# A transformer block on one core: the router's weights made stationary, and matmuls whose result nobody reads put around a stage change

## The chip, the cores and the metric

The kernel runs on one core of one Trainium2 chip. The metric is the device time of one execution in microseconds (us). Three runs of the kernel before took 631.16, 630.52 and 634.32 us, a median of 631.16 us. The program is one launch; nothing of the computation is done on the host beyond laying out the inputs.

## What is computed

One block on x of shape (2048, 256), all in 32-bit floats:

```python
h = layernorm(x) * (1 + ca) + sa
x = x + ga * attention(h)          # 16 heads of 16, windows of 64 queries on 128 keys
h = layernorm(x) * (1 + cb) + sb
x = x + gb * ffn(h)

# router of ffn, for every token:
g = h @ rg_w.T; u = h @ ru_w.T                 # 16 experts, 256 -> 16 each
scores = abs(u * silu(g)); probs = softmax(scores)
idx = top_k(probs + extra_bias, 4); w = 1 + probs[idx] * extra_scale
# y = sum over the 4 experts of w_e * (silu(h @ wg.T) * (h @ wu.T)) @ wd.T, plus one shared expert
```

The masked softmax of a window runs over the 128 keys of the window's own and the preceding 64 positions. All matrices of the experts are 176 wide, the shared one 352.

## The kernel before, in words

**Three stages**, each a block of its own with an instruction stream for each engine; a block begins when every engine has finished the one before.

1. `project_qkv`: normalises x, transposes it on TensorE, and multiplies by the query, key and value weights in eight groups of 256 tokens. Queries and keys go to DRAM (`q_scr`, `k_scr`) and come back in another layout. TensorE's loop is `for_groups`; at its end it has nothing more to do, while SyncE still waits for the last stores and loads (`qk_st`, `qk0_ld`).
2. `attention_and_routing`: 16 tiles of 128 queries (n = 0 to 15). A program written out by hand sets the order on every engine; there is no planner. For a tile, four times (q = 0 to 3, four heads each), TensorE makes scores with queries as columns (`SB`), VectorE takes the row maxima from them (L908), TensorE transposes the maxima (L1178, tile `Y`), ScalarE copies them (`max_out`, L741), SyncE writes them by a DMA into a row of `MM`, and then TensorE makes the transposed scores (`TB`, L1160 and L1162), ScalarE takes the exponential (`exps`, L781), and TensorE multiplies by the values (`weigh`, L1172, tile `O`). The scores of the next tile are made among these. After that a tile's output is normalised, transposed (`transpose_o`, L1183), split in a high and a low part (`o_hi`, `o_lo`) and projected (`project_out`, by the helper at L109), into the same bank `Y` that takes the transposed maxima.
   Each pair of tiles is routed two pairs later: in an odd tile its normalised rows are transposed (L1196, bank `X`), in the next even tile they are split (`h2_hi`, `h2_lo`), `router` multiplies them by the router's weights, ScalarE takes an exponential (`router_exp`, L764), VectorE goes on (`route_scores`), and in the odd tile after it VectorE chooses the experts and TensorE counts ranks (`ranks`, L1210 and L1211). GpSimd sends the rows to `xs_scr` by indirect DMAs (L144). Even tiles with a router are n = 4, 6, ..., 14, six of them; the last two pairs are routed behind the loop.
3. `experts_and_output`: 96 steps of 128 rows on the experts, then 16 tiles of the shared expert.

**What sets the order around the change.** On ScalarE an even tile is: `h2_hi`, `exps(0)`, `exps(1)`, `o_hi`, `router_exp` part 0, `spread(n + 2)` (L775, it lays out queries for a later tile; only where n is at most 13), `exps(2)`, `max_out(n + 1)`, `spread`, `exps(3)`, `router_exp` part 1. On TensorE it is: scores, `router`, `transpose_o`, `weigh(0)`, `scores_t(2)`, `transpose_max(n + 1)`, `weigh(1)`, `project_out`, `scores_t(3)`, `weigh(2)`, `weigh(3)`, scores. Both engines work strictly in this order. `project_out` waits for `max_out(n + 1)`, since both use the bank `Y`:

```python
            weigh(n, 1)
            if runs(n, 1):
                if more:
                    eng.wait_ge(mt_cp, n + 2)
                project_out(m)
```

The products in high and low parts are made by `three` (L109): high by high, low by high, high by low. The router's twelve matmuls have the tokens as the stationary operand (128 columns of weights loaded for each) and 32 columns of router weights moving.

Of the kernel before, what the change touches and what calls it, by code (L numbers as in the profile page):

```python
# [12 lines left out]
P = 128  # L13
# [25 lines left out]
W_GU, W_DN = KD * 2 * FI, 2 * D  # L39
TB_PAD, TB_COL = 2, 20  # L40
L1_OPS, L2_OPS = 16, 16
R_OPS, P_OPS, RP_OPS = 20, 4, 9
W_EXP = W_GU + W_DN
HW = D + 2 * NE
# [522 lines left out]
        for_groups(eng, group)  # L567


def attention_and_routing(nc, A, T, ctx, own):  # L570


# [3 lines left out]
    def sb(name, shape, dt=F32):  # L576
        return ctx.enter_context(nc.sbuf_tensor(name, shape, dt))
# [7 lines left out]
    def sems(name, n):  # L585
        return [sem(f"{name}{i}") for i in range(n)]

    ident, iota_e, mod, VW, QC, K2, MM = [T[x] for x in ("ident", "iota_e", "mod", "VW", "QC", "K2", "MM")]
    mask_key, mask_qry, tri, r_hl, esc, wo_hl = [T[x] for x in ("mask_key", "mask_qry", "tri", "r_hl", "esc", "wo_hl")]
    half = T["half"]  # L590


    Q2 = [sb(f"Q2_{i}", [VALID + 1, HEADS, 2, CH], F32R) for i in range(4)]
# [13 lines left out]
    xn2 = sb("xn2", [P, 2, D])  # L607
    h2t = sb("h2t", [P, 2, D])
    h2T = sb("h2T", [P, 2, 2, KD, P], F32R)
    rt = sb("rt", [P, 10, 2, NE])  # L610
    rw = sb("rw", [P, 2, 2, NE])
    r_sm = sb("r_sm", [P, 3, 2])
# [29 lines left out]
    ln2_dve, ln2_act, ln2_mod, h2_ready = [sem(x) for x in ("ln2_dve", "ln2_act", "ln2_mod", "h2_ready")]  # L642
    th2_mm, h2T_hi, h2T_lo = sem("th2_mm"), sem("h2T_hi"), sem("h2T_lo")
    x1_st, h2_st = sems("x1_st", 4), sems("h2_st", 2)
    r_mm, r_act, r_dve, r_pool, rank_mm, p_dve = [sem(x) for x in ("r_mm", "r_act", "r_dve", "r_pool", "rank_mm", "p_dve")]
    cnt_mm, cnt_cp, tb, col_mm, step_tab = [sem(x) for x in ("cnt_mm", "cnt_cp", "tb", "col_mm", "step_tab")]
    block = ctx.enter_context(nc.Block())
# [88 lines left out]
    def _(eng):  # L736
# [18 lines left out]
        def h2_hi(p):  # L755
            eng.wait_ge(th2_mm, p + 1)
            eng.activation(h2T[:, 0], X[:, :].rearrange("p (a k x) -> p a k x", a=2, k=KD), ACT.Copy).then_inc(h2T_hi, 1)

        def router_exp(g, part):

            if part == 0:
                eng.wait_ge(r_mm, g + 1)
                v = X[:, 0:4 * NE].rearrange("p (a u x) -> p a u x", a=2, u=2)
                eng.activation(rt[:, 0, :, :], v[:, :, 0, :], ACT.Exp, scale=-1.0).then_inc(r_act, 1)  # L764
            else:
                eng.wait_ge(r_dve, R_OPS * g + 7)
                eng.activation(rt[:, 6, :, :], rt[:, 5, :, :], ACT.Exp).then_inc(r_act, 1)
# [20 lines left out]
        def tile(n, t, e, i):  # L788
            even = t % 2 == 0
            ahead = runs(n, 0, TILES - 3)  # L790
            if even and runs(n, 4):
                h2_hi(e - 2)
            exps(n, 0)
            if ahead and not even:
                spread(n + 2, (t + 2) % 4, 0, e + 1)
            exps(n, 1)
            if runs(n, 1):
                o_hi(n - 1)
            if even and runs(n, 4):
                router_exp(e - 2, 0)  # L800
            if ahead and even:
                spread(n + 2, (t + 2) % 4, 0, e + 1)
            if not even and runs(n, 3):
                normalise_x1(e - 1, (t // 2 + 1) % 2)
            exps(n, 2)
            if runs(n, 0, TILES - 2):
                max_out(n + 1, e + t % 2, (t + 1) % 2)
            if ahead:
                spread(n + 2, (t + 2) % 4, 1, e + 1)
            exps(n, 3)  # L810
            if even and runs(n, 4):
                router_exp(e - 2, 1)

        each_tile(tile)
        h2_hi(PAIRS - 2)
        o_hi(LAST)
        router_exp(PAIRS - 2, 0)
        router_exp(PAIRS - 2, 1)

# [2 lines left out]
        load_raw(eng, A, T, FIRST + 4, NE - 1, T["w_rest"])  # L822
        normalise_x1(PAIRS - 1, 1)
        h2_hi(PAIRS - 1)
        router_exp(PAIRS - 1, 0)
        router_exp(PAIRS - 1, 1)

# [71 lines left out]
    def _(eng):  # L899
# [66 lines left out]
        def route_scores(g):  # L966

            c = Chain(eng, r_dve, R_OPS * g)
            v = X[:, 0:4 * NE].rearrange("p (a u x) -> p a u x", a=2, u=2)

            eng.wait_ge(r_act, 2 * g + 1)
            c.mark(eng.tensor_scalar(rt[:, 1, :, :], rt[:, 0, :, :], 1.0, None, ALU.add)).wait()
            c.mark(eng.reciprocal(rt[:, 2, :, :], rt[:, 1, :, :])).wait()
            c.mark(eng.tensor_tensor(rt[:, 3, :, :], v[:, :, 0, :], rt[:, 2, :, :], ALU.mult)).wait()
            c.mark(eng.tensor_tensor(rt[:, 4, :, :], v[:, :, 1, :], rt[:, 3, :, :], ALU.mult)).wait()
            c.mark(eng.scalar_tensor_tensor(out=rt[:, 9, :, :], in0=rt[:, 4, :, :], scalar=-1.0, in1=rt[:, 4, :, :],
                                            op0=ALU.mult, op1=ALU.max)).wait()
            c.mark(eng.tensor_reduce(r_sm[:, 0, :], rt[:, 9, :, :], AX.X, ALU.max, negate=True)).wait()
            c.mark(eng.tensor_tensor(rt[:, 5, :, :], rt[:, 9, :, :], b3(r_sm[:, 0, :]), ALU.add))
            assert c.k == 7  # L980
# [153 lines left out]
    def _(eng):  # L1134
# [62 lines left out]
            mm.then_inc(th2_mm, 1)  # L1197

        def router(g):
            eng.wait_ge(h2T_lo, g + 1)  # L1200
            for a in range(2):
                mm = three(eng, X[:, a * 2 * NE:(a + 1) * 2 * NE],
                           [(h2T[:, 0, a, k, :], h2T[:, 1, a, k, :], r_hl[:, k, 0, :], r_hl[:, k, 1, :]) for k in range(KD)])
            mm.then_inc(r_mm, 1)

        def ranks(g, par):

            eng.wait_ge(r_dve, R_OPS * g + R_OPS)
            for a in range(2):
                eng.matmul(X[:, a * NE:(a + 1) * NE], tri[:, 0, :], mask_e[:, par, a, :], start=True, stop=False)  # L1210
                mm = eng.matmul(X[:, a * NE:(a + 1) * NE], tri[:, 1, :], msum[:, par, a, :], start=False, stop=True)  # L1211
            mm.then_inc(rank_mm, 1)

        eng.nop(nofuse=True).then_inc(rank_mm, 1)
        eng.wait_ge(q_spread, 2)
        for q in range(4):
            scores(0, 0, q)
# [5 lines left out]
        def tile(n, t, e, i):  # L1223
# [18 lines left out]
                transpose_o(m)  # L1242
            weigh(n, 0)
            scores_t(n, t, 2)
            if more:
                if runs(n, 1):
                    eng.wait_ge(oT_lo, m + 1)
                else:
                    eng.wait_ge(mt_cp, n + 1)
                transpose_max(n1, (t + 1) % 2)  # L1250
# [26 lines left out]
        transpose_o(LAST)  # L1277
        router(PAIRS - 2)
        project_out(LAST)
        ranks(PAIRS - 2, 0)  # L1280
        eng.wait_ge(p_dve, P_OPS * (PAIRS - 2) + 1)
        transpose_h2(PAIRS - 1, 1)
        router(PAIRS - 1)
        ranks(PAIRS - 1, 1)
        eng.wait_ge(p_dve, P_OPS * (PAIRS - 1) + 1)
        eng.matmul(X[:, 0:NE], tri[:, 1, :], msum[:, 0, 0, :], start=True, stop=True).then_inc(cnt_mm, 1)
# [514 lines left out]
def program(nc, A, out):  # L1801
    with ExitStack() as keep:
# [23 lines left out]
        with ExitStack() as shared:  # L1826
            for name, shape, dt in (("mod", [P, 4, D], F32), ("esc", [P, 2, NE], F32),
                                    ("mask_key", [MASKS + 1, P], F32R), ("mask_qry", [MASKS, P], F32R),
                                    ("tri", [P, 2, P], F32R), ("r_hl", [P, KD, 2, 2 * NE], F32R),
                                    ("wo_hl", [P, KD, 2, D], F32R), ("half", [P, 2], F32),  # L1830
                                    ("QC", [VALID + 1, HEADS, 2, CH], F32R)):
                T[name] = shared.enter_context(nc.sbuf_tensor(name, shape, dt))
            for name, shape in (("K2", [VALID + 1, HEADS, WIN]),
# [14 lines left out]
def constants():  # L1848
# [12 lines left out]
    tris[:, 0, :] = np.triu(np.ones((P, P)), 1)  # L1861
    tris[:, 1, :] = 1
    halves = (np.arange(P)[:, None] // DH % 2 == np.arange(2)[None, :]).astype(np.float32)
    e = np.arange(NE, dtype=np.float32)
    iotas = np.broadcast_to(np.stack([e, e * CAP]), (P, 2, NE))
    w = np.arange(P)[:, None]
# [54 lines left out]
```

## Time and profile before

| | |
|---|---|
| median of three runs | 631.16 us |
| the profiled execution | 636.92 us, its span 635.1 us |
| mean granted TensorE clock | 0.891 of full speed |
| TensorE matmul busy | 515.7 us (81%) in 3587 instructions |
| VectorE busy | 397.5 us (63%) |
| ScalarE busy | 279.0 us (44%) |
| GpSimd busy | 293.1 us (46%) |

Times in the rows are in us from the start of the span; "x8" is a count of instructions merged into one row. The end of a matmul is modelled and overlaps the next one's start, so the cost of a group in a packed stream is the distance from its start to the next start. A float32 matmul (both operands plain f32, such as `weigh`) stands in the trace as two instructions. The clock is a share of TensorE's full 2.4 GHz, so 0.50 is 1.2 GHz. "L109" is line 109, here a helper's.

### The profile page before, as it was taken

How to read it: one execution, taken by the hardware profiler on the slowest of the kernel's cores; microseconds unless marked ns; L12 is line 12 of the kernel's file. 1: busy time of each engine (PE TensorE's matmuls, PEld its weight loads, DVE VectorE, ACT ScalarE, POOL GpSimd, SP SyncE). 2: the span in 40 equal slices, each digit the busy share in tenths (PEclk: the TensorE clock that was granted, in tenths of full speed). 3: DMA queues.
4: the chain of work that ended last, by engine and by line, in shares of the span. 5: the costliest groups of instructions: out<-in, count | busy, mean ns of one | idle time of the engine just before them, and what ended most of it. 6: DMA issues, size and time to landing. Idle time of an engine off the chain costs nothing. (4 is left out here: it accounts for less than half of the span.)

```text
span 635.1 us, 13356 instructions
## 1 busy us (share of the span) xinstructions
PE 515.7 (81%) x3587; PEld 486.0 (77%) x3588; DVE 397.5 (63%) x1148; ACT 279.0 (44%) x739; POOL 293.1 (46%) x338
## 2 busy tenths in 40 slices
PE   1597991999999999999733007999999999999895
PEld 0297891898989889898632007999899899998895
DVE  3697731325467877877854674677677677764653
ACT  1243543243454454453300565555565555543231
POOL 5644520100104545546557597444344344447794
PEclk9887996579699999999955557999999999999999
DMA  7135688339655646542375562444444444446941
GB/s 220 48 107 170 212 208 238 97 115 228 171 139 165 182 129 188 158 128 83 86 235 180 195 195 64 114 134 127 120 126 123 123 123 123 128 155 234 415 155 51
DMA packets 63818, 98.29 MB, mean 155 GB/s; under 512 B 10074, under 2 KB 48857, under 8 KB 62425
## 3 DMA queue, kind: packets, MB, share of 16 engines
q1 hardware_dynamic: 51195, 60.76, 35.4%
q0 software_dynamic: 8816, 31.01, 12.9%
q10 hardware_dynamic: 3758, 5.93, 3.2%
q8 instruction: 23, 0.38, 0.2%
q14 instruction: 26, 0.21, 0.1%
HBM read 60.84 MB, written 40.17 MB: 159 GB/s over the span
## 5 line engine op out<-in xcount | busy, mean ns | idle before, releaser
L144 POOL DMA_INDIRECT xs_scr<-h,slot_u x64 | 70.2, 1097 | 64.1 <-PE TB L1162 26.7
L109 PE MATMUL GU<-gu_hi,xT 128*128 x320 | 86.0, 351 | 3.3 <-POOL lo L1543 2.3
L1605 DVE TENSOR_TENSOR h_act<-GU,g_act 128x176 f32<-128x176 f32 (+1 forms) x96 | 35.7, 372 | 64.5 <-ACT g_act L1466 64.5
L1172 PE MATMUL O<-raw,prob 128*128 128x99 f32 x512 | 71.2, 289 | 0.0
L109 PE MATMUL YP<-dn_hi,aT 88*128 x320 | 68.5, 307 | 0.9 <-DVE aT L1598 0.9
L781 ACT ACTIVATE prob<-TB 128x512 f32<-128x512 f32 x64 | 38.2, 597 | 69.6 <-PE TB L1162 68.9
L1172 PEld LDWEIGHTS O<-raw,prob 128*128 128x128 f32 x512 | 66.7, 205 | 0.0
L1473 ACT ACTIVATE aT<-HT 88x256 fp32r<-88x256 f32 (+1 forms) x96 | 38.2, 399 | 64.4 <-PE HT L1717 64.4
L1561 POOL DMA_INDIRECT ys_scr<-y_st,ids_st x40 | 38.5, 961 | 55.2 <-DVE y_st L1613 55.0
L1561 POOL DMA_INDIRECT ys_scr<-h,ids_st x40 | 38.4, 959 | 52.1 <-DVE h L1613 50.9
L1707 PE MATMUL XT<-ident,x_st 128*128 128x128 f32 x192 | 38.1, 282 | 26.8 <-DMA x_st<-xs_scr 26.2
L109 PEld LDWEIGHTS GU<-gu_hi,xT 128*128 128x128 f32 x320 | 53.5, 195 | 4.9 <-issue 4.7
L109 PEld LDWEIGHTS YP<-dn_hi,aT 88*128 88x128 f32 x320 | 48.9, 191 | 5.6 <-issue 1.2
L109 PE MATMUL GU<-lo,xT 128*128 x160 | 52.8, 330 | 0.0
L908 DVE TENSOR_REDUCE neg_m<-SB 128x4 f32<-128x512 f32 x64 | 42.1, 687 | 16.4 <-PE SB L1150 16.0
L1466 ACT ACTIVATE g_act<-GU 128x176 f32<-128x176 f32 (+1 forms) x96 | 32.8, 341 | 44.4 <-PE GU L109 43.8
L1598 DVE TENSOR_TENSOR aT<-HT,aT 88x256 fp32r<-88x256 f32 (+1 forms) x96 | 42.5, 443 | 14.1 <-ACT aT L1473 4.6
L1707 PEld LDWEIGHTS XT<-ident,x_st 128*128 128x128 f32 x192 | 27.1, 144 | 30.8 <-DMA x_st<-xs_scr 27.0
L1150 PEld LDWEIGHTS SB<-K,Q 97*128 97x128 f32 x256 | 43.6, 214 | 3.4
L109 PE MATMUL YP<-lo,aT 88*128 x160 | 45.1, 282 | 0.0
L1162 PEld LDWEIGHTS TB<-Q,K 97*128 97x128 f32 x256 | 41.9, 206 | 3.2
L1593 DVE TENSOR_TENSOR xT<-XT,xT 128x256 fp32r<-128x256 f32 x96 | 40.6, 423 | 4.8 <-ACT xT L1460 4.7
(200 smaller groups left out, 1237.2 us busy)
## 6 DMA issues: line engine op xcount, KB each, us to landing
x_st<-xs_scr SPq DMA_DIRECT2D x80, 144.0 KB
K<-k_scr SPq DMA_DIRECT2D x48, 192.0 KB, 3.6
planes<-ys_scr POOLq DMA_DIRECT2D x8, 1024.0 KB, 17.0
k_scr<-k_ev SPq DMA_DIRECT2D x8, 768.0 KB, 4.9
QC<-q_scr SPq DMA_DIRECT2D x24, 256.0 KB, 4.4
q_scr<-q_ev SPq DMA_DIRECT2D x8, 512.0 KB, 3.0
raw<-in_egu SPq DMA_DIRECT2D x9, 352.0 KB
raw<-in_x SPq DMA_DIRECT2D x36, 64.0 KB, 2.9
```

Source lines behind the costliest of these rows:

```text
L109: mm = eng.matmul(out, a, b, start=(i + j == 0), stop=(i == len(pairs) - 1 and j == 2))
L144: eng.indirect_dma_start(T["xs_scr"], bass.IndirectOffsetOnAxis(ap=T["slot_u"][:, par, t % 2, k:k + 1], axis=0), T["h2"][:, t, :], None).t ...
L781: eng.activation(prob[:, q, :], TB[q % 2][:, :], ACT.Exp, scale=SCALE).then_inc(exp_done, 1)
L908: eng.tensor_reduce(neg_m[:, p2, 4 * q:4 * q + 4], SB[q % 2][:, :].rearrange("p (h x) -> p h x", h=4), AX.X, ALU.max, negate=True).then_in ...
L1150: mm = eng.matmul(bank[:, hh * P:(hh + 1) * P], queries(t, 4 * q + hh), keys(par, 4 * q + hh, j), start=False, stop=True, skip_group_check ...
L1162: mm = eng.matmul(bank[:, hh * P:(hh + 1) * P], keys(par, 4 * q + hh, j), queries(t, 4 * q + hh), start=False, stop=True, skip_group_check ...
L1172: mm = eng.matmul(O[:, head // 8, at:at + WIDE * VC], prob[:, q, hh * P:(hh + 1) * P], VW[:, bass.ds(HEADS * n + head, WIDE), :].rearrange ...
L1473: eng.activation(aT[0:rows, p2, 0, 0:k, :], HT[p2][0:rows, 0:k * P].rearrange("p (k x) -> p k x", k=k), ACT.Copy).then_inc(aT_hi, 1)
L1561: eng.indirect_dma_start(ys, bass.IndirectOffsetOnAxis(ap=ids_st[:, r:r + 1].bitcast(U32), axis=0), results(r % 8), None).then_inc(sent[q] ...
L1593: eng.tensor_tensor(xT[:, p2, 1, :, :], XT[p2][:, 0:D].rearrange("p (k x) -> p k x", k=KD), xT[:, p2, 0, :, :].bitcast(F32), ALU.subtract) ...
L1598: eng.tensor_tensor(aT[0:rows, p2, 1, 0:k, :], HT[p2][0:rows, 0:k * P].rearrange("p (k x) -> p k x", k=k), aT[0:rows, p2, 0, 0:k, :].bitca ...
L1707: mm = eng.transpose(XT[t % 2][:, k * P:(k + 1) * P], x_st[:, t, k * P:(k + 1) * P], ident[:, :])
```

## The change

Four things are edited; the rest of the kernel is as it was.

- At the end of stage 1 TensorE makes 40 matmuls of 512 columns into the bank `TH[0]`, which nobody reads any more, with weights that lie in SBUF. At the start of stage 2 it makes 8 of 512 columns into `X` before it waits for the first queries.
- The router's weights become the stationary operand (64 columns: high and low parts of both matrices) and the tokens move, 256 columns in a matmul: four matmuls for each pair, with all four products of high and low parts. The result (64 x 256) is copied to SBUF by ScalarE (`router_out`), and two plain f32 matmuls (`router_back`) with a 0/1 matrix turn it back to tokens by 32 and add high and low up.
- `router_back` stands behind `scores_t(2)` on TensorE. On ScalarE `router_out` stands ahead of `o_hi`, and `router_exp` stays where it was.
- The rank matmuls take both tiles of a pair at once: two of 32 columns in place of four of 16.

```diff
 STREAM_1, STREAM_2 = 40, 8
...
         for_groups(eng, group)
+        for _ in range(STREAM_1):
+            eng.matmul(TH[0][:, :], w_hl[:, 0, 0, 0:P], w_hl[:, 0, 0, 0:512], start=True, stop=True)
...
+        def router_out(g):
+            eng.wait_ge(rl_mm, g + 1)
+            if g >= 1:
+                eng.wait_ge(r_mm, g)
+            eng.activation(rl[:, :], X[0:4 * NE, 0:2 * P], ACT.Copy).then_inc(rl_cp, 1)
...
             exps(n, 1)
+            if even and runs(n, 4):
+                router_out(e - 2)
             if runs(n, 1):
                 o_hi(n - 1)
             if even and runs(n, 4):
...
         h2_hi(PAIRS - 1)
+        router_out(PAIRS - 1)
         router_exp(PAIRS - 1, 0)
...
         def router(g):
             eng.wait_ge(h2T_lo, g + 1)
+            for k in range(KD):
+                for l in range(2):
+                    mm = eng.matmul(X[0:4 * NE, 0:2 * P].rearrange("p (a x) -> p a x", a=2),
+                                    r_hl[:, k, :, :].rearrange("p l x -> p (l x)"), h2T[:, l, :, k, :],
+                                    start=(k + l == 0), stop=(k + l == KD))
+            mm.then_inc(rl_mm, 1)
+
+        def router_back(g):
+            eng.wait_ge(rl_cp, g + 1)
             for a in range(2):
-                mm = three(eng, X[:, a * 2 * NE:(a + 1) * 2 * NE],
-                           [(h2T[:, 0, a, k, :], h2T[:, 1, a, k, :], r_hl[:, k, 0, :], r_hl[:, k, 1, :]) for k in range(KD)])
+                mm = eng.matmul(X[:, 2 * P + 2 * NE * a:2 * P + 2 * NE * (a + 1)], rl[:, a * P:(a + 1) * P], both,
+                                start=True, stop=True)
             mm.then_inc(r_mm, 1)
...
             eng.wait_ge(r_dve, R_OPS * g + R_OPS)
-            for a in range(2):
-                eng.matmul(X[:, a * NE:(a + 1) * NE], tri[:, 0, :], mask_e[:, par, a, :], start=True, stop=False)
-                mm = eng.matmul(X[:, a * NE:(a + 1) * NE], tri[:, 1, :], msum[:, par, a, :], start=False, stop=True)
-            mm.then_inc(rank_mm, 1)
+            v = X[:, 0:2 * NE].rearrange("p (a x) -> p a x", a=2)
+            eng.matmul(v, tri[:, 0, :], mask_e[:, par], start=True, stop=False)
+            eng.matmul(v, tri[:, 1, :], msum[:, par], start=False, stop=True).then_inc(rank_mm, 1)
...
+        for _ in range(STREAM_2):
+            eng.matmul(X[:, :].rearrange("p (h x) -> p h x", h=4), mask_qry[:, :],
+                       mask_key[0:MASKS, :].unsqueeze(1).broadcast_to([MASKS, 4, P]), start=True, stop=True)
         eng.wait_ge(q_spread, 2)
...
             weigh(n, 0)
             scores_t(n, t, 2)
+            if even and runs(n, 4):
+                router_back(e - 2)
             if more:
```

The constant matrix `both` adds 32 columns to the small tensor `half`.

## Rows read from the trace of the kernel before

**Rows 1.** Windows: TensorE, its weight loads, VectorE, ScalarE, GpSimd; clock, DMA share, GB/s
```profile
97.20:100.60 3.40, 0.00 (x0) 0.00 (x0) 0.19 (x1) 0.60 (x3) 0.00 (x0) 1.00 1.11 345
100.60:110.50 9.90, 0.00 (x0) 0.00 (x0) 2.17 (x6) 4.02 (x8) 0.00 (x0) 0.51 0.71 199
110.50:134.80 24.30, 23.47 (x97) 22.04 (x97) 5.92 (x10) 6.95 (x10) 2.21 (x4) 0.50 0.37 108
134.80:158.60 23.80, 22.59 (x178) 21.48 (x177) 13.29 (x32) 9.95 (x17) 0.95 (x1) 1.00 0.74 181
158.60:168.90 10.30, 10.30 (x48) 9.89 (x46) 3.21 (x11) 5.31 (x9) 2.55 (x2) 0.51 0.47 123
168.90:315.70 146.80, 136.86 (x1096) 130.27 (x1094) 111.13 (x364) 67.72 (x123) 66.87 (x104) 1.00 0.53 144
```

**Rows 2.** Timeline (start, length, engine, line), change from stage 1 to 2
```profile
94.19 2.98 PE L109 MATMUL VB<-w_hl,hT 128*128 128x256 f32 x24
...
102.61 0.58 SPq L286 DMA_DIRECT2D k_scr<-k_ev  x1
...
108.31 4.26 ACT L775 ACTIVATE Q<-QC,half 97x1024 fp32r<-97x1024 f32 x4 [5.88 <-PEq L1836]
...
110.54 0.79 PE L1147 MATMUL SB<-mask_key,mask_qry 126*128 126x512 f32 x1 [13.37 <-ACT Q L775]
```

**Rows 3.** Timeline, first tiles of stage 2
```profile
111.88 0.74 PE L1147 MATMUL SB<-mask_key,mask_qry 126*128 126x512 f32 x1
...
116.71 0.38 PE L1178 MATMUL Y<-ident,neg_m 128*16 128x128 f32 x1 [0.78 <-DVE neg_m L908]
...
117.13 0.27 ACT L741 ACTIVATE mT<-Y 16x128 fp32r<-16x128 f32 x1 [4.56 <-PE Y L1178]
...
119.41 0.79 PE L1160 MATMUL TB<-MM,mask_key 127*128 127x512 f32 x1
...
135.84 0.45 PE L1160 MATMUL TB<-MM,mask_key 127*128 127x512 f32 x1
...
145.95 0.44 PE L1160 MATMUL TB<-MM,mask_key 127*128 127x512 f32 x1
```

**Rows 4.** Waits of TensorE (us in total, times, longest), whole span
```profile
PE Y L1178 <- DVE oT L926: 5.8, 5, 1.2
...
PE TB L1160 <- DMA MM<-mT: 1.2, 1, 1.2
```

**Rows 5.** Timeline of TensorE, the even tile n = 6
```profile
199.40 1.46 PE L109 MATMUL X<-r_hl,h2T 128*128 128x32 f32 x12
200.71 0.44 PE L1183 MATMUL Y<-ident,o_n 128*128 128x128 f32 x2
...
201.79 0.48 PE L1160 MATMUL TB<-MM,mask_key 127*128 127x512 f32 x1
...
202.62 1.03 PE L1172 MATMUL O<-raw,prob 128*128 128x99 f32 x8
203.50 0.98 PE L109 MATMUL Y<-wo_hl,oT 128*128 128x256 f32 x6
```

**Rows 6.** Timeline of ScalarE, the same tile
```profile
201.46 0.19 ACT L764 ACTIVATE rt<-X 128x32 f32<-128x32 f32 x1
201.54 1.15 ACT L775 ACTIVATE Q<-QC,half 97x1024 fp32r<-97x1024 f32 x1
202.70 0.60 ACT L781 ACTIVATE prob<-TB 128x512 f32<-128x512 f32 x1
203.19 0.25 ACT L741 ACTIVATE mT<-Y 16x128 fp32r<-16x128 f32 x1
```

**Rows 7.** Timeline, routing of the last pair and end of stage 2
```profile
333.26 1.26 POOL L847 TENSOR_TENSOR h<-h2t,mod 128x512 f32<-128x512 f32 x1 [4.10 <-DMA xs_scr<-h,slot_u]
...
337.16 2.74 PE L109 MATMUL X<-r_hl,h2T 128*128 128x32 f32 x12 [1.41 <-DVE h2T L960]
...
353.71 0.41 DVE L1072 CAST step_i<-X 1x256 int32<-1x256 f32 x1 [1.10 <-PE X L1289]
```

More of the change, by code:

```diff
@@ L41 @@
 L1_OPS, L2_OPS = 16, 16
+STREAM_1, STREAM_2 = 40, 8
 R_OPS, P_OPS, RP_OPS = 20, 4, 9
@@ L589, in attention_and_routing @@
     mask_key, mask_qry, tri, r_hl, esc, wo_hl = [T[x] for x in ("mask_key", "mask_qry", "tri", "r_hl", "esc", "wo_hl")]
-    half = T["half"]
+    half, both = T["half"], T["half"][0:4 * NE, 2:2 + 2 * NE]
     Q2 = [sb(f"Q2_{i}", [VALID + 1, HEADS, 2, CH], F32R) for i in range(4)]
@@ L609, in attention_and_routing @@
     h2T = sb("h2T", [P, 2, 2, KD, P], F32R)
+    rl = sb("rl", [4 * NE, 2 * P])
     rt = sb("rt", [P, 10, 2, NE])
@@ L644, in attention_and_routing @@
     x1_st, h2_st = sems("x1_st", 4), sems("h2_st", 2)
+    rl_mm, rl_cp = sem("rl_mm"), sem("rl_cp")
     r_mm, r_act, r_dve, r_pool, rank_mm, p_dve = [sem(x) for x in ("r_mm", "r_act", "r_dve", "r_pool", "rank_mm", "p_dve")]
@@ L762, in router_exp @@
                 eng.wait_ge(r_mm, g + 1)
-                v = X[:, 0:4 * NE].rearrange("p (a u x) -> p a u x", a=2, u=2)
+                v = X[:, 2 * P:2 * P + 4 * NE].rearrange("p (a u x) -> p a u x", a=2, u=2)
                 eng.activation(rt[:, 0, :, :], v[:, :, 0, :], ACT.Exp, scale=-1.0).then_inc(r_act, 1)
@@ L816, in _ @@
         o_hi(LAST)
+        router_out(PAIRS - 2)
         router_exp(PAIRS - 2, 0)
@@ L968, in route_scores @@
             c = Chain(eng, r_dve, R_OPS * g)
-            v = X[:, 0:4 * NE].rearrange("p (a u x) -> p a u x", a=2, u=2)
+            v = X[:, 2 * P:2 * P + 4 * NE].rearrange("p (a u x) -> p a u x", a=2, u=2)
             eng.wait_ge(r_act, 2 * g + 1)
@@ L1279, in _ @@
         project_out(LAST)
+        router_back(PAIRS - 2)
         ranks(PAIRS - 2, 0)
@@ L1283, in _ @@
         router(PAIRS - 1)
+        router_back(PAIRS - 1)
         ranks(PAIRS - 1, 1)
@@ L1829, in program @@
                                     ("tri", [P, 2, P], F32R), ("r_hl", [P, KD, 2, 2 * NE], F32R),
-                                    ("wo_hl", [P, KD, 2, D], F32R), ("half", [P, 2], F32),
+                                    ("wo_hl", [P, KD, 2, D], F32R), ("half", [P, 2 + 2 * NE], F32),
                                     ("QC", [VALID + 1, HEADS, 2, CH], F32R)):
@@ L1863, in constants @@
     halves = (np.arange(P)[:, None] // DH % 2 == np.arange(2)[None, :]).astype(np.float32)
+    both = np.arange(P)[:, None] % (2 * NE) == np.arange(2 * NE)[None, :]
+    halves = np.concatenate([halves, both.astype(np.float32)], 1)
     e = np.arange(NE, dtype=np.float32)
```

## The prediction

> **What bounds the kernel now.** I read the windows first, cut where the granted clock changes. TensorE is busy nearly all of the attention, so there its speed sets the pace, and its clock is not always full: it is still 1.00 for the first 3.4 us after the last product of stage 1, then half of full (1.2 GHz) while the engine does nothing, and it stays half for 24.3 us of stage 2, though TensorE is busy for 23.47 of them. It falls once more for 10.3 us, and then holds for 146.8 us [rows 1]. The timeline of the stage change shows why TensorE idles: its last product ends at 97.17, but the last store of keys is issued at 102.61, with the DMA engines full, and stage 2 opens at 108.31, when ScalarE starts the first queries; TensorE waits for them until 110.54 [rows 1, 2]. From there, a unit of time saved on TensorE's order, or on what it waits for, moves everything behind it: the last step of stage 2 (353.71) and stage 3 follow by the same amount. The waits say what else binds: five waits of about 1.2 us for VectorE's low part of the output, in odd tiles, and one of 1.2 us for the DMA of the maxima [rows 4]. In even tiles TensorE waits for nothing.
>
> **Stream 1.** 24 products of 256 columns took 2.98 us, 0.124 each, so one of 512 is about 0.25 and 40 are 9.9 us: 97.2 to 107.1. They end ahead of 108.31, lie beside the DMAs and cost nothing; 1.2 us of idling remain, less than the 3.4 us that the clock outlasted [rows 1, 2]. The Trainium skill (TensorE: Matmul & The Clock Gate, Back-to-back issue gap) gives columns over 2.4 GHz plus 2.5 ns for one matmul alone, 0.216 us; by that the stream ends at 105.8 and 2.5 us remain idle. No row shows 512 columns back to back, and the gap is still the shorter one, so the sum is the same and only the chance of a fall grows. If the stream took longer than 11 us, stage 2 would open late; at 0.25 each it can't.
>
> **Stream 2.** Eight at 0.25 are 2.0 us, 108.3 to 110.3, ahead of the queries' 110.54: nothing. At half clock twice that, 4.0, the first scores start at 112.3: +1.8 us [rows 2].
>
> **The start of the attention at full clock.** Two pieces. (a) From 110.54 to the transposed maxima is 6.17 us. VectorE's four reductions set part of this and don't get faster, TensorE's part halves: I take 3.9 us, since a group of scores goes from 1.34 (110.54 to 111.88) to at most 0.8 (the like group from 201.79) and the last reduction still follows the last group [rows 3, 5]. The way of the maxima by ScalarE and the DMA (116.71 to 119.41, 2.7 us) hardly shrinks. So the transposed scores start at 117.0 in place of 119.41: -2.4 us. Bounds: 0, if VectorE sets it all, and -3.1, half of the 6.17. (b) Tile 0 took 119.41 to 135.84, 16.4 us. Tile 1, at full clock, took 135.84 to 145.95, 10.1 us, with a transpose and an output projection (about 0.27 and 0.82 on TensorE) that tile 0 has not: 9.2 us with a little left for a wait on ScalarE. So -7.2 us [rows 3]. Together **-9.6 us**. A check from above: 97 matmuls in 24.3 us would take 13.0 at the 7.5 per us of the stretch that follows, -11.3 [rows 1]. What is late next are the DMAs of the first weights, which are queued tile by tile behind the same maxima; the DMA share was 0.37 in this stretch [rows 1], so they fit.
>
> **The router in an even tile.** Before: twelve products, 199.40 to 200.71, 1.31 us. After: four of 256 columns at 0.124, 0.50 us. The stationary operand has 64 columns, no more than in those rows. Then transpose, `weigh(0)` and the transposed scores follow as they did, 0.8 us earlier, the next thing after the scores being due at 201.69. There stands `router_back`: two f32 products, four instructions, at 0.11 each (eight of `weigh` fill 202.62 to 203.50), 0.44 us [rows 5]. Bounds 0.1 and 0.5. TensorE alone would gain 0.37 us. But ScalarE's queue counts. Its exponential for the router now waits for `router_back` (result at 202.3), and behind it stand the spread (1.15 us), `exps(2)` and the copy of the maxima, for which the projection waits. Before, the exponential started at 201.46 and the projection at 203.50, 0.06 us after that copy ended: 2.04 us from one to the other [rows 5, 6]. After: 202.3 + 2.04 = 204.34. TensorE would have been ready at 203.1, so it stands for 1.2 us and the projection is **0.84 us late**. What follows (`exps(3)`, VectorE's normalising, the odd tile) hangs on TensorE, and all is late by this. Five tiles have the spread (n = 4 to 12): +4.2 us. In n = 14 there is none, and the 0.37 is gained. `router_out` (64 x 256, at most the 0.6 us of the 128 x 512 exponential [rows 6]) lies beside `weigh(0)` and delays `o_hi` by less than that product takes; its cover gone it would add that to every even tile. Bounds of the tile: -0.37 (ScalarE has slack) to +1.3.
>
> **Ranks.** Four become two: -0.22 us at 0.11 each, in six odd tiles, where TensorE goes on from its wait for VectorE to the tile's end: -1.3 us. That VectorE's choice might be what they wait for bounds it at 0.
>
> **Behind the loop.** The last pair's router starts when GpSimd's rows, held back by its own sends, are there (333.26), so what came before is not on the path by itself, but from here on everything is serial and at half clock. Before 2.74 us. After: 4 x 0.25, result 0.2 later, copy 0.4, 4 x 0.22 and 0.2 again: 2.7 us, no change, bounds -0.5 and +0.8. The ranks save 2 x 0.22 = 0.4 [rows 7, 5].
>
> **Sum**: -9.6 + 4.2 - 0.4 - 1.3 - 0.4 = -7.5 us on a profiled 636.92, so 629.4. The median of the runs, 631.16, lies 5.8 lower; part of that is perhaps the second stretch at half clock (48 matmuls in 10.3 us, 6.4 at the rate before it: 3.9 us [rows 1]), part a shorter first one, so 1 us less is to be had there: -6.5, **624.7 us**. I call 1% (6.3 us) what a measurement tells from no change.
>
> **Rivals.** (1) *ScalarE is no obstacle* and the router gives its full 0.37 in six tiles: -9.6 - 2.2 - 1.3 - 0.4 = -13.5, with the 1 us off 618.7. For it: it is what moving the work by 0.8 us earlier suggests. Against: the projection already started 0.06 us behind ScalarE's copy [rows 5, 6]. (2) *The clock is lost at the start.* In tile 0 the maxima's way leaves TensorE idle for some 1.1 us of 2.7 even at full clock, with 0.5 to 1 us of waits for VectorE just before; a wait of 1.2 us before 157.6 was followed by a fall at 158.6, while five equal ones later were not [rows 1, 3, 4]. Then 2.4 of the 9.6 remain, or none of them and +1.8 of stream 2: 631 to 635, say 632. (3) *One fall more* in an even tile's new wait: -6.5 + 3.9, 628.6. (4) **The side that is slower**: the new waits of 1.2 us in the five even tiles take the clock down again and again, where before only odd tiles had such waits. Each fall costs 3.9 us; the gain is gone from the second on, and four give -6.5 + 15.6 = +9.1, 640. Against it: the five old waits did nothing of the kind in 146.8 us. The Trainium skill (TensorE: Matmul & The Clock Gate, A second HAM failure mode) describes a kernel in which short idling between groups of matmuls made the clock swing. By that rule (4) would be the likely case; the trace shows it once in six waits.
>
> **Chances.** Forecast 0.45 (its own range 621 to 628, of which 0.30 lies below 624.8), (1) 0.13, (2) 0.17, (3) 0.15, (4) 0.10. Faster by over 1%: 0.30 + 0.12 = 0.42. Slower by over 1%: (4), 0.10. Within: the rest, 0.48. The range for 8 in 10 reaches from 617.5, most of (1), to 634.5, most of (2), and leaves (4) out. The unknown prices (start 0 to -11, even tile -0.37 to +1.3) lie within.
>
> **What would show it.** Granted clock 1.00 from 97 to 135, stream 1 ending before 107.5 and the first scores no later than 110.6; the transposed scores of tile 0 near 117.0 and of tile 1 near 126.2. In even tiles n = 4 to 12 a wait of TensorE for ScalarE's copy of the maxima ahead of the projection, near 1.2 us, and a pair of tiles longer by 0.6 us; in n = 14 none. The cast that ends stage 2 comes 7.5 us earlier. I would be wrong if the clock drops near 109 or 117, if that wait is absent, or if stage 3 changes by itself.

## The result: the block became slower

The kernel after takes 642.86 us (median of four runs, 641.85 to 643.32), the kernel before, run beside it, 631.25 us (630.52 to 634.32): 1.0186 of before, 95% interval 1.0140 to 1.0232. Forecast were 624.7 us and a range of 617.5 to 634.5, so the sign was wrong and the time lies outside the range.

The two profiled executions are closer together: 636.92 us before, 641.85 after (spans 635.1 and 640.0), +4.9. The rest of the 11.6 is no work that the traces show: the profiled execution of before lies 5.7 above its median, that of after 1.0 below its own. In 73 later runs the kernel before took 626 to 639 us, with medians of 635.6 to 636.3 in three comparisons. Against those 642.86 would be about 1.011; the kernel after itself was not repeated, so the loss can be put at 1 to 2% and not closer. What follows is read against runs of before in the same comparison. The medians given are those of all runs, while the ratios leave out every run more than 1.5% above the fastest of its kernel, which strips before of its slower runs wherever one of them was very fast.

Windows of after, cut where the granted clock changes (columns as in [rows 1], which they answer to):

```profile
99.10:108.20 9.10, 9.10 (x41) 7.19 (x39) 2.28 (x5) 2.45 (x6) 0.00 (x0) 1.00 0.99 281
108.20:111.40 3.20, 0.05 (x1) 0.03 (x1) 0.07 (x1) 0.17 (x1) 0.00 (x0) 0.99 0.67 217
111.40:114.80 3.40, 3.40 (x8) 2.72 (x9) 0.00 (x0) 3.40 (x4) 0.64 (x1) 0.51 0.01 2
114.80:121.40 6.60, 4.77 (x32) 4.04 (x31) 4.11 (x6) 0.96 (x2) 1.56 (x4) 1.00 0.73 210
121.40:152.10 30.70, 29.81 (x127) 28.46 (x128) 6.26 (x12) 9.01 (x14) 0.00 (x0) 0.50 0.27 75
152.10:322.80 170.70, 155.63 (x1220) 146.34 (x1219) 124.23 (x398) 80.52 (x147) 70.63 (x107) 1.00 0.56 150
```

The stream of stage 1 holds the clock at 1.00, and it stays there while TensorE is idle for 3.2 us. It falls just ahead of the first product of stage 2, is back when those eight products end, and falls again in the stretch cut at 121.4. From there TensorE is busy for 29.81 of 30.70 us and stays at 1.2 GHz all the while. Before had 24.3 and 10.3 us at half in this part of stage 2, after has 3.4 and 30.7: as much, in other places.

Timeline of after, the change of stage and the first tiles (start, length, engine, line), which answers to [rows 2, 3]:

```profile
98.96 9.29 PE L572 MATMUL TH<-w_hl 128*128 128x512 f32 x40
105.54 0.58 SPq L287 DMA_DIRECT2D k_scr<-k_ev  x1
111.23 4.27 ACT L789 ACTIVATE Q<-QC,half 97x1024 fp32r<-97x1024 f32 x4 [5.86 <-PEq L1872]
111.41 3.63 PE L1245 MATMUL X<-mask_key,mask_qry 126*128 126x512 f32 x8 [3.15 <-PEq L1872]
114.88 0.39 PE L1165 MATMUL SB<-mask_key,mask_qry 126*128 126x512 f32 x1
...
118.81 0.28 PE L1196 MATMUL Y<-ident,neg_m 128*16 128x128 f32 x1 [0.78 <-DVE neg_m L926]
...
122.29 0.80 PE L1178 MATMUL TB<-MM,mask_key 127*128 127x512 f32 x1 [1.83 <-DMA MM<-mT]
```

Three things are to be seen. Stage 2 opens at 111.23, 2.9 us later than before. The eight products of stream 2, at half clock, end at 114.88, 1.4 us after the queries would have let the scores start (2.23 us behind the opening, as before). And the second fall lies within the 1.83 us that TensorE waits for the DMA of the maxima; 1.65 us of products stand between this wait and the one of 0.78 us for VectorE's last reduction.

**Where the 4.9 us are.** First transposed scores 119.41 to 122.29, +2.9, all of it the later opening: from there to these scores it is 11.1 us in both, so that the 1.4 us of late scores are made up. Tiles 0 to 3: 16.4, 10.1, 11.6, 15.2 became 17.2, 16.0, 10.3, 11.2, together +1.3: tile 1 now runs cold, tile 3 no longer does. Tiles 4 to 14: 131.0 to 133.9, +2.9. From the start of tile 15 to the last cast (353.71, now 359.78): -1.0. Stage 3, 281.4 to 280.2: -1.2. (A tile's time is the distance between its first transposed scores and those of the next.)

TensorE and ScalarE of after in the even tile n = 6, which answers to [rows 5, 6]:

```profile
204.12 0.64 PE L1222 MATMUL X<-h2T,r_hl 128*64 128x256 f32 x4
...
205.63 0.48 PE L1178 MATMUL TB<-MM,mask_key 127*128 127x512 f32 x1
...
206.44 0.63 PE L1231 MATMUL X<-half,rl 64*128 64x32 f32 x4
...
209.02 0.98 PE L110 MATMUL Y<-wo_hl,oT 128*128 128x256 f32 x6 [0.87 <-ACT mT L749]
```

```profile
207.10 0.20 ACT L778 ACTIVATE rt<-X 128x32 f32<-128x32 f32 x1 [1.66 <-PE X L1231]
207.20 1.14 ACT L789 ACTIVATE Q<-QC,half 97x1024 fp32r<-97x1024 f32 x1
208.24 0.59 ACT L795 ACTIVATE prob<-TB 128x512 f32<-128x512 f32 x1
208.71 0.25 ACT L749 ACTIVATE mT<-Y 16x128 fp32r<-16x128 f32 x1
```

ScalarE waits 1.66 us for `router_back`, and the spread, the exponential and the copy of the maxima stand behind it. From the router to the projection it is 4.90 us, where it was 4.10. The waits of TensorE, whole span, say how often (us in total, times, longest); this answers to [rows 4]:

```profile
PE Y L110 <- ACT mT L749: 4.4, 5, 0.9
PE Y L1196 <- DVE oT L944: 6.1, 6, 1.1
PE X L1245 <- PEq L1872: 3.2, 1, 3.2
```

### The profile page after: what moved, and what is told of

Its sections match the earlier page's. It is cut to its first block and busy times, and to the rows that moved or that the text cites. A ratio compares the mean times of both kernels' runs of the same rounds, so it can differ in the third digit from the quotient of the medians.

```text
span 640.0 us, 13371 instructions
## 1 busy us (share of the span) xinstructions
PE 519.5 (81%) x3587; PEld 485.2 (76%) x3588; DVE 397.6 (62%) x1148; ACT 281.3 (44%) x747; POOL 292.6 (46%) x338
## 5 line engine op out<-in xcount | busy, mean ns | idle before, releaser
L110 PEld LDWEIGHTS GU<-gu_hi,xT 128*128 128x128 f32 x320 | 52.9, 192 | 4.8 <-issue 4.7
L110 PE MATMUL QB<-hT,w_hl 128*128 128x256 f32 (+1 forms) x192 | 33.0, 332 | 14.5 <-DVE hT L446 10.7
L1168 PEld LDWEIGHTS SB<-K,Q 97*128 97x128 f32 x256 | 41.6, 204 | 3.2
```

The source lines that it names most:

```text
L110: mm = eng.matmul(out, a, b, start=(i + j == 0), stop=(i == len(pairs) - 1 and j == 2))
L1168: mm = eng.matmul(bank[:, hh * P:(hh + 1) * P], queries(t, 4 * q + hh), keys(par, 4 * q + hh, j), start=False, stop=True, skip_group_check ...
```

## The experiments

Two theories stood after this look. **A**: the loss has three separate parts, a later opening of stage 2 (from the longer `half`, since no other edit runs before stream 1 and the second store of keys is already issued at another time, 49.74 for 51.82), a wait in each of five even tiles, and a clock that the streams don't hold. **B**, the rival: the streams cost the time (TensorE's products beside the last stores, or the extra 2 us), and the router is neutral. (The expectations name theories by their own letters: there the late opening is A, later A1, the wait in the even tiles C, and the clock that isn't held B.)

### One part of the change at a time

`half_only`: the kernel before with the longer tensor, nobody reads the new columns.

```diff
-("half", [P, 2], F32),
+("half", [P, 2 + 2 * NE], F32),
+    both = np.arange(P)[:, None] % (2 * NE) == np.arange(2 * NE)[None, :]
+    halves = np.concatenate([halves, both.astype(np.float32)], 1)
```

> Only the 32 added columns of the constant tensor half (34 instead of 2 in a row), nothing of the streams, the router or the ranks. Theory A (the wider tensor moves what lies behind it, and with it the pace at which stage 1's stores reach DRAM): the stores of keys follow each other at 8.2 to 8.8 us as in the changed kernel, not at 7.4 to 7.8 as before, stage 2 opens about 3 us later, the time is 3 to 5 us above the kernel before. Rival (the slower stores come from TensorE's added matmuls or from one execution to the next): the pace and the time stay as before, within 1 us.

Measured: 638.67 us beside 636.31 for before, 1.0060 (1.0012 to 1.0108); by the medians 2.4 us, where 3 to 5 were expected. Stage 2 opens at 110.98 in place of 108.31. So 2.7 of the 2.9 us of delay are there, with no stream and no router.

`streams_only`: the kernel before with both loops of unread products.

```diff
+STREAM_1, STREAM_2 = 40, 8
+        for _ in range(STREAM_1):
+            eng.matmul(TH[0][:, :], w_hl[:, 0, 0, 0:P], w_hl[:, 0, 0, 0:512], start=True, stop=True)
+        for _ in range(STREAM_2):
+            eng.matmul(X[:, :].rearrange(...), mask_qry[:, :], mask_key[...], start=True, stop=True)
```

> The kernel before with both groups of unread matmuls and nothing else. Theory B (the clock does not hold in stage 2: it falls in the wait for the maxima of tile 0, and only some 2 us of the head are won): between -2 and +3 us against the kernel before. Rival (the streams alone are worth the 9.6 us of the prediction and the loss is the router's): 6 to 10 us faster. Second rival (the streams themselves do harm, by a stretch at half clock that lasts longer than the old one): 4 us or more slower.

Measured: 634.87 us, 0.9991 (0.9921 to 1.0060): neither gain nor loss, within the -2 to +3 us expected. (One of its ten runs took 1170.47 us, and one of `stream48` below 661.95; no trace of these was taken.) Its two streams:

```profile
98.30 9.29 PE L571 MATMUL TH<-w_hl 128*128 128x512 f32 x40
110.61 3.75 PE L1220 MATMUL X<-mask_key,mask_qry 126*128 126x512 f32 x8 [3.02 <-PEq L1843]
```

TensorE idles for 3.0 us between them, the clock falls near 110.0, after 2.4 us of it, and stays at half for 41 us. That the streams by themselves cost the whole loss is out; that they hold the clock is out too. They aren't quite free, though: from the issue of the seventh store of keys to the opening it is 18.7 us here, and 18.7 to 18.9 in all seven traces with a stream behind stage 1, but 17.9 to 18.3 in the seven without one.

`router_only`: the kernel after without the two loops.

```diff
-        for _ in range(STREAM_1):
-            eng.matmul(TH[0][:, :], ...)
-        for _ in range(STREAM_2):
-            eng.matmul(X[:, :]..., ...)
```

> The changed kernel without both groups of unread matmuls: stationary router, merged ranks, wider half. Theory C (the router's wait for ScalarE in five even tiles, 0.9 us each, less 0.2 us in six odd tiles, plus the slower stores): 5 to 8 us slower than the kernel before, 3 of them before stage 2 opens. Rival (the router part is a gain and the streams do the harm): 1 to 3 us faster.

Measured: 641.54 us, 1.0128 (1.0037 to 1.0219), within what was expected. This holds the loss of the change; it includes the longer `half`. Even tiles last 12.2 us as in after, but for one:

```profile
257.82 1.48 PE L110 MATMUL Y<-wo_hl,oT 128*128 128x256 f32 x6 [0.87 <-ACT mT L747]
```

Right behind this new wait of 0.87 us the clock falls at 258.0, for 3.4 us, and the tile (n = 10) takes 13.8 us, 1.6 more than the others.

`exp_behind_max`: the kernel after with ScalarE's exponential of the router behind its copy of the maxima.

```diff
-            if even and runs(n, 4):
-                router_exp(e - 2, 0)
...
+            if even and runs(n, 4):
+                router_exp(e - 2, 0)
```

> The changed kernel with one move: on ScalarE the router's first exponential stands behind the copy of the maxima instead of ahead of the spread. Theory C: TensorE's five waits of 0.9 us ahead of the output projection go, the time falls by 4 to 5 us against the changed kernel (642.9), to about 638. Rival (the wait moves elsewhere, to VectorE's route scores or to the odd tile): within 1.5 us of the changed kernel.

Measured: 635.86 us, 1.0010 (0.9945 to 1.0075), 5.7 us under `router_only` in the same comparison. The same stretch of ScalarE and TensorE in this kernel:

```profile
205.44 0.60 ACT L795 ACTIVATE prob<-TB 128x512 f32<-128x512 f32 x1
206.21 0.27 ACT L749 ACTIVATE mT<-Y 16x128 fp32r<-16x128 f32 x1 [0.17 <-PE Y L1196]
206.38 0.17 ACT L778 ACTIVATE rt<-X 128x32 f32<-128x32 f32 x1
```

```profile
203.01 0.64 PE L1222 MATMUL X<-h2T,r_hl 128*64 128x256 f32 x4
...
206.82 0.96 PE L110 MATMUL Y<-wo_hl,oT 128*128 128x256 f32 x6
```

Router to projection is 3.81 us, without the wait; and TensorE has no wait for the copy of the maxima left. Even tiles 6 to 12 take 11.1 us, 0.3 less than before the change (tile 4 still 12.15). The five even tiles together fell from 61.2 to 56.6 us, the odd ones between and behind them from 63.0 to 61.6, and the way from opening to last cast from 248.5 to 242.6. So the loss in the even tiles comes from ScalarE's order, shown by its removal.

### What in the longer tensor costs the opening

`half_sbuf` (first diff): the columns in SBUF only, two are loaded as before. `half_dram` (second diff): in DRAM only, where the input is as wide as in `half_only`. Both are the kernel before otherwise.

```diff
-        eng.dma_start(T["half"][:, :], A["halves"]).then_inc(k_ld, 16)
+        eng.dma_start(T["half"][:, 0:2], A["halves"]).then_inc(k_ld, 16)
-("half", [P, 2], F32),
+("half", [P, 2 + 2 * NE], F32),
```

```diff
-        eng.dma_start(T["half"][:, :], A["halves"]).then_inc(k_ld, 16)
+        eng.dma_start(T["half"][:, :], A["halves"][:, 0:2]).then_inc(k_ld, 16)
```

> The kernel before with half 34 columns wide in SBUF alone; the input in DRAM stays 2 wide. Theory A1 (what counts is where the tensors behind it lie in SBUF, among them q_ev and k_ev, from which stage 1's stores read): the stores of keys come 8.2 to 8.8 us apart as in half_only, stage 2 opens near 111, the time is 2 to 4 us over the kernel before. Theory A2 (the place of the DRAM tensors counts): 7.3 to 7.8 us apart and the time unchanged within 1 us.

> The kernel before with the input halves 34 columns wide in DRAM alone; SBUF stays as it was. Theory A1: stores 7.3 to 7.8 us apart, no change within 1 us. Theory A2: 8.2 to 8.8 us apart and 2 to 4 us slower.

Two consecutive stores of keys in stage 1, first in before, then in after, then in `half_sbuf`, then in `half_dram`:

```profile
82.50 0.58 SPq L286 DMA_DIRECT2D k_scr<-k_ev  x1
90.35 0.58 SPq L286 DMA_DIRECT2D k_scr<-k_ev  x1
```

```profile
83.57 0.58 SPq L287 DMA_DIRECT2D k_scr<-k_ev  x1
92.38 0.58 SPq L287 DMA_DIRECT2D k_scr<-k_ev  x1
```

```profile
83.94 0.58 SPq L286 DMA_DIRECT2D k_scr<-k_ev  x1
92.75 0.58 SPq L286 DMA_DIRECT2D k_scr<-k_ev  x1
```

```profile
82.96 0.58 SPq L286 DMA_DIRECT2D k_scr<-k_ev  x1
90.77 0.58 SPq L286 DMA_DIRECT2D k_scr<-k_ev  x1
```

With the columns in SBUF a group of stage 1 takes 8.8 us here, without them 7.8. (Not every distance grows: the first is 11.0 us with them and 12.6 to 12.9 without, so that of some 4.4 us in the later ones 2.5 are left at the last store.) `half_sbuf` opens stage 2 at 110.75 and took 638.67 us beside 635.59, 1.0111 (1.0016 to 1.0205); `half_dram` opens it at 108.79. So it is the room in SBUF, not the transfer. `half_dram` took 635.83 us, 0.2 us over the median of before, as its pace lets one expect. Its ratio of 1.0071 (1.0016 to 1.0126) looks like a loss, but it sets all ten of its runs against the faster eleven of the nineteen of before.

`half_wider` tells whether any room will do: 64 columns (256 bytes in each partition) in place of 32 (128 bytes), two loaded.

```diff
-("half", [P, 2], F32),
+("half", [P, 2 + 4 * NE], F32),
```

> The kernel before with half 66 columns wide in SBUF alone, so what lies behind it moves twice as far as in half_sbuf. If it is the distance to an alignment of 256 bytes that slows the stores: 7.3 to 7.8 us apart and no change in time. If any move from the old place slows them, or a coarser alignment counts: 8 us or more apart and 2 to 4 us slower.

```profile
81.98 0.58 SPq L286 DMA_DIRECT2D k_scr<-k_ev  x1
89.78 0.58 SPq L286 DMA_DIRECT2D k_scr<-k_ev  x1
```

Measured: 635.08 us beside 635.99, 0.9997 (0.9963 to 1.0030), and the old pace is back, 7.8 us, stage 2 opens at 107.78. What counts is where the tensors behind `half` come to lie: 128 bytes on, the stores are slower, 256 bytes on, they aren't, as the first case of the expectation had it. The stores' median from issue to landing goes with it: 4.9 us before, 5.5 in after and `half_sbuf`, 4.7 here. What this costs in time is 2 to 3 us by the medians of `half_only` and `half_sbuf`. Which of the tensors it is, and why, stays open.

`router_built`: `exp_behind_max` without streams, with `half` as before and the 0/1 matrix made on the chip in a tensor of its own, allotted last.

```diff
+    both = sb("both", [4 * NE, 2 * NE])
...
+        eng.tensor_tensor(both[:, :], ident[0:4 * NE, 0:2 * NE], ident[0:4 * NE, 2 * NE:4 * NE], ALU.add).then_inc(both_set, 1)
```

> Stationary router, merged ranks and the router's exponential behind the copy of the maxima; no unread matmuls; the 0/1 matrix is made on VectorE in stage 2 from the identity, so half is 2 wide in SBUF and DRAM. If theories A and C are both right, stage 1 keeps the old pace (7.3 to 7.8 us a store, stage 2 opens near 108), even tiles take 11.1 us (before 11.4) and odd ones 0.2 less, and the whole is 3 to 4 us faster than the kernel before. Rival (what moves the stores is another part of the change, the layout of stage 2's tensors or its code): stores 8.2 to 8.8 us apart and no gain.

Measured: 630.72 us beside 635.59, 0.9968 (0.9925 to 1.0011). Opening at 107.90, and 240.5 us from there to the last cast, where before takes 245.4 us; the clock falls in the same two places in both, and the even tiles take 11.1 us. The interval touches 1, but the medians lie 4.9 us apart and 14 of the 19 runs of before took longer than the slowest of these ten (633.50), so the router's gain is likely.

### What holds the clock

`stream48`: the kernel before with both streams, the first lengthened to 48. It closes most of the idle time at the change of stage and leaves the waits for the first maxima open.

```diff
+STREAM_1, STREAM_2 = 48, 8
```

> The kernel before with 48 and 8 unread matmuls at the stage change and none in the waits behind. It tells which open wait took the clock. If it is the one at the stage change: holds, 622 to 627 us, tile 0 in 9 to 10 us. If it is the wait for the first maxima (theory B as predicted): the clock is full at the first scores and falls between 114 and 122, tile 0 takes 16 to 17 us, 632 to 637 us.

`clock_fill`: the same, and unread products in those waits too.

```diff
+STREAM_1, STREAM_2, FILL_1, FILL_2 = 48, 8, 4, 8
...
         for q in range(4):
             scores(0, 0, q)
+        for _ in range(FILL_1):
+            eng.matmul(X[:, :]..., mask_qry[:, :], mask_key[...], start=True, stop=True)
         transpose_max(0, 0)
         eng.wait_ge(q_spread, 4)
         scores(1, 1, 0)
         scores(1, 1, 1)
+        for _ in range(FILL_2):
+            eng.matmul(X[:, :]..., mask_qry[:, :], mask_key[...], start=True, stop=True)
```

> The kernel before with unread matmuls alone, more of them: 48 behind stage 1, 8 at the start of stage 2, 4 ahead of the first transposed maxima and 8 behind the second group of tile 1's scores, so that TensorE has no wait of over 1 us up to the transposed scores of tile 0. Theory B (the clock fell because those waits were left open): it holds at full up to tile 2, tile 0 takes 9 to 10 us in place of 16 to 17, the time is 6 to 10 us under the kernel before. Rival (the clock falls in the attention whatever stands before it): tile 0 takes over 15 us and the time is 0 to 5 us above.

Windows of `stream48`, then the products behind its two waits up to the fall, then windows of `clock_fill` (columns as above):

```profile
98.10:109.20 11.10, 11.08 (x50) 8.80 (x48) 2.28 (x5) 2.44 (x6) 0.00 (x0) 1.00 0.99 293
109.20:112.50 3.30, 2.10 (x9) 1.45 (x9) 0.07 (x1) 2.27 (x3) 0.00 (x0) 1.00 0.01 4
112.50:116.30 3.80, 3.15 (x20) 2.68 (x20) 2.59 (x4) 2.00 (x2) 2.22 (x4) 1.00 0.45 112
116.30:136.80 20.50, 18.50 (x78) 17.44 (x78) 3.53 (x7) 4.87 (x8) 0.00 (x0) 0.50 0.37 107
```

```profile
110.40 2.09 PE L1220 MATMUL X<-mask_key,mask_qry 126*128 126x512 f32 x8 [1.22 <-PEq L1843]
...
116.53 0.38 PE L1182 MATMUL Y<-ident,neg_m 128*16 128x128 f32 x1 [0.79 <-DVE neg_m L912]
```

```profile
96.30:107.40 11.10, 11.08 (x50) 8.80 (x48) 2.28 (x5) 2.44 (x6) 0.00 (x0) 1.00 0.99 291
107.40:119.60 12.20, 9.56 (x51) 7.49 (x51) 4.18 (x7) 4.54 (x5) 2.21 (x4) 1.00 0.47 126
119.60:301.40 181.80, 172.34 (x1381) 164.73 (x1381) 126.46 (x407) 87.22 (x154) 69.98 (x106) 1.00 0.56 153
```

`stream48`, 635.42 us, 1.0003 (0.9962 to 1.0043), as expected if the wait for the first maxima takes the clock: it comes through the change of stage, with 1.2 us of idling left, and falls near 116.4, in the wait of 0.79 us for VectorE's last reduction and ahead of that for the DMA of the maxima. `clock_fill`, 623.52 us beside 635.59 (620.83, 623.16, 623.87 and 635.87), 0.9878 (0.9755 to 1.0001), more than the 6 to 10 us expected; the interval from four runs touches 1, but three of them lie below all 19 of before (626.46 and up). Full clock until 301.4. Its TensorE there:

```profile
108.65 2.08 PE L1220 MATMUL X<-mask_key,mask_qry 126*128 126x512 f32 x8 [1.27 <-PEq L1849]
...
113.83 1.15 PE L1226 MATMUL X<-mask_key,mask_qry 126*128 126x512 f32 x4
114.81 0.27 PE L1182 MATMUL Y<-ident,neg_m 128*16 128x128 f32 x1
...
116.26 2.06 PE L1233 MATMUL X<-mask_key,mask_qry 126*128 126x512 f32 x8
...
119.64 0.50 PE L1164 MATMUL TB<-MM,mask_key 127*128 127x512 f32 x1 [1.32 <-DMA MM<-mT]
...
128.81 0.45 PE L1164 MATMUL TB<-MM,mask_key 127*128 127x512 f32 x1
```

Tile 0 takes 9.17 us, where 16.43 were needed; but the first transposed scores start at 119.64, no earlier than before (119.41): the maxima are transposed 1.9 us earlier, and the way from there by ScalarE and the DMA takes 4.8 us in place of 2.7. The DMA is issued at 115.47, and its data are awaited until 119.64. The traces show what goes with it: SyncE issues three loads of queries (`QC`, 256 KB each) ahead of the 8 KB of maxima. In before the maxima are issued 4.9 us behind the first of these loads and land 1.9 us later; in `clock_fill` they are issued 2.7 us behind it and land 4.1 us later. In none of the fourteen traces do they land less than 6.6 us behind that load, however early TensorE makes them. That they stand behind the loads is likely; no run moved them.

Part of the gain of `clock_fill` may not be the fillers': it has no second stretch at half clock either (10.3 us in before, tile 3 in 15.3 us, 10.6 here), and `half_sbuf` and `stream48` have none too.

`after_fill` puts the same four counts into the kernel after, `all_good` into `router_built`:

```diff
-STREAM_1, STREAM_2 = 40, 8
+STREAM_1, STREAM_2, FILL_1, FILL_2 = 48, 8, 4, 8
```

> The changed kernel with only the unread matmuls extended (48, 8, 4, 8); wide half and ScalarE's order as in the change. Theory B: the clock holds up to tile 2 and the time falls by 8 to 12 us against the changed kernel (642.9), to 631 to 635, with even tiles still at 12.2 us and the stores 8.2 to 8.8 us apart. Rival (stage 2 opens later here, the 48 end too early and the clock falls before it): tile 0 in over 15 us, 640 or more.

> The stationary router and merged ranks with the router's exponential behind the copy of the maxima, the 0/1 matrix made in stage 2 (half 2 wide), and the unread matmuls in four places (48, 8, 4, 8). If the three causes are separate and add up: stores 7.3 to 7.8 us apart, tile 0 in 9 to 10 us, even tiles 11.1 us; against the kernel before -3 to -4 from the router and -8 to -12 from the clock, together 618 to 623 us where before has a median of 636. Rival (they interfere, the clock falls again in the shorter tiles): 625 or more.

`after_fill`: 632.24 us beside 635.99, 0.9940 (0.9897 to 0.9982), within 631 to 635 as expected; tile 0 takes 9.2 us there too, stage 2 still opens late and even tiles still last 12.2. Its clock falls once, at 154.2 for 6.8 us, right behind a wait of 1.50 us for the DMA of tile 3's maxima. `all_good`: 0.9791 (0.9704 to 0.9877), from three runs of 617.33, 618.67 and 625.25 us; 618 to 623 was expected. Its trace joins what the parts gave: full clock, no late opening (108.8), even tiles of 11.1 us and a way of 228.8 us from the opening to the last cast, where before takes 245.4. Three further runs of it, which the ratio leaves out, took 632 to 633 us with a mean clock of 0.903 to 0.908 against 0.918 to 0.928 in the first three, so the median of all six is 628.72 us beside 635.99; even these three lie below that median of before. One of the four of `clock_fill` was like that (635.87, 0.906) and one of the ten of `after_fill` (640.34, 0.906). No trace of such a run was taken. Whether the hold failed in them is open, and whoever uses this version has to reckon with them.

## Why the prediction was wrong

**The step that failed: the start of the attention at full clock**, -9.6 us, the largest term. The 40 and 8 products did not keep the clock. It was given as rival (2), *the clock is lost at the start*, with a chance of 0.17 and the right place, the way of the maxima: `stream48` bridges the change of stage and loses the clock there all the same, `clock_fill` fills it and keeps the clock. In after it fell even before, at the change of stage, where 3.15 us were left to idle and not 1.2. What the argument took from too little: that before could idle 3.4 us at 1.00 [rows 1] was to cover any shorter idle time. It doesn't: `streams_only` lost the clock 2.4 us behind its stream, the kernel after 3.1 us behind its own, and `stream48` in a wait of 0.79 us that came some 5 us behind one of 1.22. After's second stretch at half clock lasted 30.7 us with TensorE busy for 97% of them, so tile 1 ran at half clock as well, and tiles 0 to 3 lost 1.3 us in all. A cold tile 1 with a warm tile 3 is not the streams' doing: `half_dram`, where only the input behind `half` is wider, has the same four tiles (17.2, 15.8, 10.4, 11.2). The Trainium skill (TensorE: Matmul & The Clock Gate, A second HAM failure mode) tells of such short idling between groups of matmuls; the prediction gave that rule to the even tiles and not to the start, where `stream48` agrees with it. In the even tiles it hardly shows: of the fifteen new waits of 0.87 us in the traces of after, `router_only` and `after_fill` one was followed by a fall, which cost 1.6 us and not the 3.9 of rival (3).

**Its two pieces.** (b), tile 0 from 16.4 to 9.2 us, is right to 0.03 us where the clock is held (`clock_fill`: 9.17). (a), the first transposed scores 2.4 us earlier, gave 0: the stated bound of 0 is what holds, though for a reason not given. The way by ScalarE and the DMA, which I let "hardly shrink", grew by 2.1 us, most likely because the maxima stand behind the loads of queries (see `clock_fill`). The check from above of -11.3 was therefore no check.

**A term that was not in the sum: the added columns of `half`.** I treated them as nothing and named no cover. They open stage 2 by 2.4 to 2.7 us later (`half_sbuf`, `half_only`), not by the transfer but by moving what lies behind them in SBUF (`half_wider`). No row of before could give that number; a bound from both sides, which each unshown cost was to have, could have held it.

**Stream 1**: 40 products in 9.29 us, 0.232 each, where 0.25 was taken. The Trainium skill (TensorE: Matmul & The Clock Gate, Back-to-back issue gap) gives 0.216 us for one alone; the trace lies above it. The stream ended at 108.2 and left 3.15 us idle, where 1.2 was said: 0.6 us is the shorter stream, and the opening moved by 2.9 us but the start of the stream only by 1.8 (98.96 for 97.2). "Cost nothing" was not quite right either: with a stream the opening comes some 0.7 us later behind the seventh store of keys. **Stream 2**: the case given for half clock came, 3.4 us, and the scores started 1.4 us late (1.8 was said), which the full clock behind them made up.

**The router in an even tile**: right. Predicted +0.84 in five tiles, a sum of 4.2; measured 11.44 to 12.23, +0.79, a sum of 4.0. The distance from ScalarE's exponential to the projection, 2.04 in the working, is 1.92. The wait itself is 0.87, predicted 1.2, as TensorE came to it 0.3 us later than worked out; `router_back`, 0.56 us and not 0.44, is 0.1 of that. `exp_behind_max` shows the cause. In n = 14 the tile gained 0.25 of 0.37.

**Ranks**: odd tiles 5 to 13 gained 0.8 together, predicted 1.1 for these five. **Behind the loop**: -1.0, predicted -0.6 with tile 15's ranks. **Stage 3** changed by itself, by -1.2 us, which the prediction named as a sign of being wrong; no run explains it, and it is small beside the spread of before.

**The sum against the profile**: predicted -7.5, measured +4.9, 12.4 apart. Up to the first transposed scores it is +2.9 for -2.4 (5.3 apart), in tiles 0 to 3 +1.3 for -7.2 (8.5), in tiles 4 to 14 +2.9 for +2.7 (0.2), in the rest of stage 2 -1.0 for -0.6 (-0.4), in stage 3 -1.2 for 0. By cause, the clock at the start makes 10.9 of it and the opening 2.9. The remaining 6.7 us up to the medians stay open, but the traces point somewhere. Of the kernels that are before but for `half` or the two streams, two were traced in an execution near 631 us (`half_sbuf` 631.4, `stream48` 630.9): the clock is back by 138 us and doesn't fall again in the attention, and tiles 0 to 3 take 48.0 and 48.1 us. Five, with before itself, were traced at 634.6 to 639.5 (`half_wider`, `streams_only`, before, `half_dram`, `half_only`): they have either a second stretch at half clock from 158 on or one first stretch that lasts past 149, and these tiles take 52.9 to 54.9 us. So one stretch at half clock more or less, which comes and goes by itself, is likely much of the spread between 628 and 639 us; before was traced only once, so this is not shown.

## What to carry to other kernels

A stream of unread products has to reach over every wait up to the point where the steady work begins: ask which wait comes next after the one that is filled, and fill or price that too. A product that returns late can cost more than its own time, namely what its consumer's queue has behind the consumer; move the consumer behind whatever another engine waits for. A tensor that grows is an edit too: when a stage with nothing changed in it gets slower, give the new data a place at the end and look again. And before a change is compared by profiles, look whether both executions had their stretches at half clock in the same places.

## What the runs showed of the hardware

- With 128 bytes more per partition ahead of the tensors of stage 1 the last of its store-bound groups took 8.8 us in place of 7.8 and the stores landed after 5.5 us in place of 4.9 (`half_sbuf`, `half_only`); with 256 bytes more it was 7.8 and 4.7 (`half_wider`).
- TensorE was busy for 29.81 of 30.70 us and stayed at 1.2 GHz; in the same trace eight 512-column products, 3.4 us, were followed by full clock. Behind stage 1 the clock fell after 3.6 us of idling in before, 3.1 in after and 2.4 in `streams_only`; in `stream48` it fell during a wait of 0.79 us.
- Back to back, a 512-column product took 0.232 us at full clock; eight at half clock 3.4 us, 0.43 each.
- 8 KB of maxima landed 1.9 us after their issue when issued 4.9 us behind the first of three loads of 256 KB (before), and 4.1 us after it when issued 2.7 us behind (`clock_fill`).
